# Latent attention: order of a score pass and the context's transposes, and operands filled up from 32 to 128 rows

## The reference, cut to what matters

```python
q = (x @ W_q).reshape(b, t, 16, 8).transpose(0, 2, 1, 3)
lat = x @ W_dkv                                   # 32 features
lat = (lat - mean) * rsqrt(var + 1e-5) * ln_gamma + ln_beta
k = (lat @ W_uk).reshape(b, t, 16, 8).transpose(0, 2, 1, 3)
v = (lat @ W_uv).reshape(b, t, 16, 8).transpose(0, 2, 1, 3)
q, k = apply_rope(q), apply_rope(k)
scores = einsum('bhqd,bhkd->bhqk', q, k) / sqrt(8)
attn = softmax(where(causal, scores, -inf))
out = einsum('bhqk,bhkd->bhqd', attn, v).transpose(0, 2, 1, 3).reshape(b, t, 128) @ W_o
```

## Time and profile before

| what | us |
|---|---|
| median of three runs | 1756.51 (1756.41 to 1758.79) |
| the profiled execution | 1753.8 |
| its span, first to last instruction | 1752.0 |
| latent layer, from the first copy to latT to the last one (15 steps) | 589.5 to 1008.3 |

### The profile page before, as it was taken

The page is one execution under the profiler, slowest core; times in us unless marked ns, Lnnn a source line. Parts: engine busy times, 40 slices in busy tenths (PEclk is TensorE's granted clock), DMA queues, the critical chain, the costliest instruction groups (busy, mean ns, idle before and its releaser), DMA issues.

```text
span 1752.0 us, 33687 instructions
## 1 busy us (share of the span) xinstructions
PE 1506.7 (86%) x12538; PEld 1127.1 (64%) x12538; DVE 1014.7 (58%) x2795; ACT 729.0 (42%) x1281; POOL 252.7 (14%) x514
## 2 busy tenths in 40 slices
PE   5999999994099499999999995499998899998977
PEld 3666666662098266666666654366665899997667
DVE  4666777764065355665666546734444566664856
ACT  0444444333065134434343333266666455553322
POOL 0000000010601212212121101200000000000423
PEclk7999999995599568887897867789999899998989
DMA  9000000000122100000000000000000000000001
GB/s 304 13 1 1 1 1 2 1 1 2 58 62 68 61 4 7 7 4 7 4 7 4 1 1 1 1 1 2 2 1 2 1 1 2 1 2 1 1 16 34
DMA packets 32673, 30.39 MB, mean 17 GB/s; under 512 B 4536, under 2 KB 29312, under 8 KB 31872
## 3 DMA queue, kind: packets, MB, share of 16 engines
q1 hardware_dynamic: 30464, 24.05, 4.5%
q0 software_dynamic: 2048, 4.20, 0.8%
HBM read 18.01 MB, written 10.22 MB: 16 GB/s over the span
## 4 chain that ended last, share of the span: by engine, by line
PE 72%; DVE 10%; POOL 5%; ACT 5%; issue 4%; DMA 2%; SPq 0%; POOLq 0%; DVEq 0%; ACTq 0%
PE S L355 12%; PE O L1559 7%; PE O L425 6%; PE S L341 5%; PE A L329 4%; PE S L344 4%; PE A L310 3%; PE A L330 3%; ACT probs L647 3%; PE O L429 3%; PE S L1541 2%; PE A L446 2%; PE S L1542 2%; PE S L1543 2%; PE O L383 2%
## 5 line engine op out<-in xcount | busy, mean ns | idle before, releaser
L647 ACT ACTIVATE probs<-S 128x1024 f32<-128x1024 f32 x288 | 290.8, 1026 | 217.8 <-PE S L355 211.9
L823 DVE TENSOR_REDUCE nm<-S 128x4 f32<-128x1024 f32 x128 | 151.8, 1215 | 88.7 <-PE S L355 88.5
L156 POOL TENSOR_TENSOR ve<-mv,eps 128x2 f32<-128x2 f32 x112 | 26.5, 237 | 1112.4 <-DVE mv L148 1112.4
L1627 ACT ACTIVATE probs<-S,eb 128x256 f32<-128x256 f32 x256 | 107.7, 474 | 117.8 <-PE S L1543 117.8
L654 ACT COPY OT<-O 128x512 f32<-128x512 f32 x96 | 56.3, 587 | 206.2 <-PE O L429 206.2
L425 PE MATMUL O<-probs,V 128*32 128x256 f32 x1536 | 134.8, 426 | 4.8 <-ACT probs L647 3.3
L1559 PE MATMUL O<-ew,probs 128*128 128x128 f32 x1024 | 138.1, 278 | 0.3 <-ACT probs L1627 0.2
L329 PE MATMUL A<-hi,spread 128*128 128x256 f32 x384 | 117.8, 335 | 18.0 <-DVE lo L802 8.8
L355 PEld LDWEIGHTS S<-QM,KS 32*128 32x128 f32 x1024 | 87.3, 223 | 69.8 <-issue 69.8
L1559 PEld LDWEIGHTS O<-ew,probs 128*128 128x128 f32 x1024 | 125.1, 192 | 5.2 <-ACT probs L1627 3.5
L355 PE MATMUL S<-QM,KS 32*128 32x256 f32 (+1 forms) x1024 | 127.3, 353 | 0.0
(11 more groups left out here) (338 smaller groups left out, 3116.4 us busy)
## 6 DMA issues: line engine op xcount, KB each, us to landing
ew<-in_w SPq DMA_DIRECT2D x2, 2048.0 KB, 10.1
moe_rows<-zeros SPq DMA_DIRECT2D x1, 2944.0 KB, 12.9
xin<-moe_rows SPq DMA_DIRECT2D x23, 128.0 KB, 2.6
ew<-in_w SPq DMA_DIRECT2D x2, 1024.0 KB
out<-X SPq DMA_DIRECT2D x16, 128.0 KB, 1.8
moe_made<-ctx_sb SPq DMA_DIRECT2D x12, 128.0 KB, 1.8
moe_made<-ctxT SPq DMA_DIRECT2D x11, 128.0 KB, 1.8
probs<-in_spread SPq DMA_DIRECT2D x1, 1024.0 KB, 5.2
```

What stands on the lines that cost most here:

```text
L647: act.activation(c.probs[:, n].rearrange("p b g l -> p b (g l)"), c.S[:, n % 2], ACT.Exp if soft else ACT.Tanh, scale=self.scale).then_inc ...
L823: dve.tensor_reduce(c.nm[:, 1, 2 * pr:2 * pr + 2, 2 * u:2 * u + 2], slot.rearrange("p b (g k) -> p b g k", g=2), AX.X, ALU.max, negate=Tru ...
L1627: act.activation(w["h"][:, x % 2, j], c.S[:, x % 2, bank, col:col + L], ACT.Relu, bias=w["b1"][:, x * self.NJ + j:x * self.NJ + j + 1]).th ...
```

## The change

It does four things, all in the latent layer. First, `latent_T` writes to bank 1 of O and not to bank 0, and the wait of `maxima` for ACT's copy of it stands ahead of the third group (the first that writes bank 1) and not ahead of the first. Second, on PE pass1(5) stands ahead of the context's transposes. Third, the two query projections change places: bank 1 of A first. Fourth, the tiles uk, uv and latT have 128 partitions; rows 32 to 127 are set to zero once at the start by six memsets on DVE, and the key and value matmuls read all 128 rows. The weight loads, the folding and ACT's copy still touch rows 0 to 31 alone, and the loads of uk and uv are issued two places later among the other loads of their group.

```diff
@@ latent_T (PE)
-                mm = pe.transpose(c.O[0:LAT, 0, t * P:(t + 1) * P], w["lat"][:, t, :], c.ident[:])
+                mm = pe.transpose(c.O[0:LAT, 1, t * P:(t + 1) * P], w["lat"][:, t, :], c.ident[:])
@@ maxima (PE)
-            if has_front and kind == "latent":
-                pe.wait_ge(e["latt"].sem, e["latt"].at(s + 1))
             for g in range(G):
+                if g == 2 and has_front and kind == "latent":
+                    pe.wait_ge(e["latt"].sem, e["latt"].at(s + 1))
                 for t in range(T):
@@ latent_step (PE)
             pass1(k, par, 4)
+            pass1(k, par, 5)
             if has_tail:
                 ctx_transposes(k - 1)
-            pass1(k, par, 5)
             if has_front:
+                projections(k + 1, 1, (0,))
                 projections(k + 1, 0, (0,))
-                projections(k + 1, 1, (0,))
                 latent_T(k + 1, nxt)
             maxima(k, has_front)
@@ latent_copy (ACT)
-            act.copy(w["latT"][:], c.O[0:LAT, 0, 0:L]).then_inc(e["latt"].sem, 1)
+            act.copy(w["latT"][0:LAT, :], c.O[0:LAT, 1, 0:L]).then_inc(e["latt"].sem, 1)
@@ build: tiles and loads
-        w1 = dict(wq=sb("wq1", [P, 2, P]), uk=sb("uk1", [LAT, 2, P]), uv=sb("uv1", [LAT, P]),
+        w1 = dict(wq=sb("wq1", [P, 2, P]), uk=sb("uk1", [P, 2, P]), uv=sb("uv1", [P, P]),
...
-                             lat=sb("lat", [P, T, LAT]), latT=sb("latT", [LAT, L]))
+                             lat=sb("lat", [P, T, LAT]), latT=sb("latT", [P, L]))
...
+        load("l1", w1["uk"][0:LAT], d["uk1"])
+        load("l1", w1["uv"][0:LAT], d["uv1"])
@@ start of DVE's program
+            for rows in (slice(LAT, 2 * LAT), slice(2 * LAT, P)):
+                dve.memset(w1["uk"][rows], 0.0).then_inc(made, 1)
+                dve.memset(w1["uv"][rows], 0.0).then_inc(made, 1)
+                dve.memset(w1["latT"][rows], 0.0).then_inc(made, 1)
```

More of the change, by code:

```diff
@@ L2283, in build @@
                              lrstd=sb("lrstd", [P, T]), lminus=sb("lminus", [P, T]), lnm=sb("lnm", [P, T]),
-                             lat=sb("lat", [P, T, LAT]), latT=sb("latT", [LAT, L]))
+                             lat=sb("lat", [P, T, LAT]), latT=sb("latT", [P, L]))
         w1["wqk"] = [w1["wq"], w1["uk"]]
-        for dst, name in ((w1["wq"], "wq1"), (w1["uk"], "uk1"), (w1["uv"], "uv1"), (w1["dkv"], "dkv1"), (w1["wo"], "wo1")):
+        for dst, name in ((w1["wq"], "wq1"), (w1["dkv"], "dkv1"), (w1["wo"], "wo1")):
             load("l1", dst[:], d[name])
+        load("l1", w1["uk"][0:LAT], d["uk1"])
+        load("l1", w1["uv"][0:LAT], d["uv1"])
         load("l1", w1["gamma"][:], d["gamma1"].rearrange("(n o) -> n o", o=1))
@@ L2373, in build @@
         experts0.loaded = loaded["moe0"], 16 * len(loads["moe0"])
-        N_MADE = 25
+        N_MADE = 31
         def fold_products(pe):
@@ L2380, in fold_products @@
             for sw in range(2):
-                pe.matmul(c.S[:, 0, 1, NE * sw:NE * sw + NE], w1["uk"][:, sw, :], w1["beta_all"][:, 0:NE], start=True, stop=True)
-            pe.matmul(c.S[:, 0, 1, P:2 * P], w1["beta_all"][:], w1["uv"][:], start=True, stop=True).then_inc(folded["beta_ps"], 1)
+                pe.matmul(c.S[:, 0, 1, NE * sw:NE * sw + NE], w1["uk"][0:LAT, sw, :], w1["beta_all"][:, 0:NE], start=True, stop=True)
+            pe.matmul(c.S[:, 0, 1, P:2 * P], w1["beta_all"][:], w1["uv"][0:LAT], start=True, stop=True).then_inc(folded["beta_ps"], 1)
         def fold(dve):
@@ L2389, in fold @@
             dve.tensor_copy(w1["bv"][:], c.S[:, 0, 1, P:2 * P]).then_inc(folded["latent_folded"], 1)
-            dve.tensor_scalar(w1["uk"][:], w1["uk"][:], w1["gamma"][:, 0:1], None, ALU.mult).then_inc(folded["latent_folded"], 1)
-            dve.tensor_scalar(w1["uv"][:], w1["uv"][:], w1["gamma"][:, 0:1], None, ALU.mult).then_inc(folded["latent_folded"], 1)
+            dve.tensor_scalar(w1["uk"][0:LAT], w1["uk"][0:LAT], w1["gamma"][:, 0:1], None, ALU.mult).then_inc(folded["latent_folded"], 1)
+            dve.tensor_scalar(w1["uv"][0:LAT], w1["uv"][0:LAT], w1["gamma"][:, 0:1], None, ALU.mult).then_inc(folded["latent_folded"], 1)
         experts0.fold_products, experts0.fold = fold_products, fold
```

## The result

The changed kernel takes 1681.12 us (median of four runs, 1675.60 to 1685.51) against 1757.65 for the kernel before (four runs, the three of the table above and 1763.98): a ratio of 0.9576, 95% interval 0.9541 to 0.9610. Forecast was 1695 with a range of 1685 to 1714. The profile after is of the quickest of the four runs (1675.60).

The account below looks back on a forecast made before the run. PE was taken to bound the kernel, with its clock falling in the latent layer. Falls 56.8 us plus maxima 4.8 made 61.6, taken from the median 1756.5: 1695 us, range 1685 to 1714.

Parts of the forecast that it names:

- The falls: Latent layer: 32-row projections let PE's clock drop to 0.50; zero rows remove 12 drops, 56.8 us; chance 0.78.
- some falls stay: Rival: 32-row score passes or PE's longer wait for lo still drop the clock; half left, 1723 us, chance 0.12.
- no fall goes: Rival: the clock follows something other than rows in use; only the maxima gain, 1747 to 1752 us, chance 0.07.
- the low clock stays longer: Rival: moved transposes or filled-up matmuls delay the clock's rise in latent steps; 31 us more, 1787, chance 0.03.
- The wait of the maxima: At L383 the maxima start after M instead of the latT copy: 0.32 us per step, 4.8 in all.
- PE's own gain: Around L310, fewer changes between 128-row and 32-row matmuls: 0 to 0.3 us per step, taken as 0.
- pass1(5): Score pass ahead of the context's transposes fills PE's 0.34 us idle, but DVE's row maxima bound it: gain 0.
- The cover on ACT: 0.32 us between ACT's later ctxT copy and lat's wait for POOL; if gone, at worst 0.3 per step, 4.5 us.
- The early step: Latent step 618.6 to 648.6, begun at low clock: left as it is; an earlier rise would give up to 6.3 us.
- the fourteenth step's fall: Latent step 1008.3 to 1037.9: without its clock drop it goes from 29.6 to 23.75 us, 5.8 less.
- the 13 steps: Latent layer, 648.6 to 1008.3, latT copy to latT copy: 359.7 us before, forecast to shorten by 55.2.

Follow-up runs that it names:

- the zero rows alone: The kernel before with only the filled-up tiles, loads and memsets; order, bank and waits as before: 1687.36 us, ratio 0.9613.
- the order alone: The changed kernel with the latent layer's key and value matmuls reading rows 0 to 31 again: 1752.93 us, ratio 0.9998.
- the cut rope layer: The changed kernel with the rope layer's keys and values contracting over 32 of 128 rows: 1749.58 us.
- 64 rows: The changed kernel with the latent layer's keys and values contracting over 64 rows instead of 128: 1696.92 us.

## Why the prediction was right in its cause and short in its sum

**The falls: right, and shown.** 32-row projections are the cause; the zero rows alone, the order alone and the cut rope layer say so in three ways. The rivals "some falls stay", "no fall goes" and "the low clock stays longer" are out for the changed kernel. The first lives in the kernels between: with 64 rows 2 steps of 13 fall.

**The wait of the maxima: right.** M to QM went from 1.33 to 1.04 us, 0.29 where 0.32 was forecast; the step gives back 0.34 with the wait put back.

**PE's own gain: taken as 0, measured 0.15 per step.** The prediction bounded it by 0 to 0.3 and said that it "would only lengthen PE's wait for lo". This step failed in its mechanism. It read DVE's chain from QM to lo as without a gap, since none of its eight rows shows idle time. There was one, too short to be printed. V ends at 709.32 + 0.48 = 709.80 and the residual L884 starts at 709.85, behind PE's output L463, which ends at 709.10 + 0.71 = 709.81:

```profile
709.32 0.48 DVE L760 TENSOR_TENSOR V<-O,bv 128x128 f32<-128x128 f32 x2
709.85 0.42 DVE L884 TENSOR_TENSOR res<-O,X 128x256 f32<-128x256 f32 x1
```

```profile
709.10 0.71 PE L463 MATMUL O<-wo,ctxT 128*128 128x128 f32 x4
```

After the change V and the residual start 0.40 apart (781.52, 781.92) and not 0.53, and the residual no longer waits: it starts before V's end at 782.00. The line of L884 as a whole hides this. It counts 16 waits before and 4 after, and none of the 16 is in the two steps at full clock; they stand in the steps with a fall and at the ends of the rope and the latent layer. So 0.13 of the 0.15 us arrives here: full rows bring PE's output earlier by 0.12 (3.90 us behind the maxima, 4.02 before), and DVE was waiting for it. From the start of QM to that of lo it is 5.18 us before (705.82 to 711.00) and 5.03 after, 5.12 in the step shown. With 64 rows V and the residual are 0.73 apart in all steps at full clock but one, and with 32-row keys 0.62, which is why their steps are longer. With the values on 32 rows PE is another 0.10 us ahead and the step stays at 23.24: only from there on is the prediction's sentence true.

**pass1(5): taken as 0, measured 0.07** per step at full clock, together with the exchange of the query projections. The prediction had DVE as the bound here. It was not quite: its maxima 4 and 5 start 1.15 us apart with the pass late and 1.11 with it early, so 0.04 of the 0.07 is another wait too short to be printed. The cover on ACT held (0.38 us).

**The early step: taken as 0, the first two gave 7.3 us** where 0.6 was forecast. In size this is the term that failed most. "I leave it as it is" put the rise of the clock at 635.1, where the kernel before had it; after, it stays up from 616.9 on, with one short rise ahead of that. Before:

```profile
589.50:635.10 45.60, 38.79 (x172) 24.13 (x172) 20.30 (x37) 8.65 (x13) 4.06 (x9) 0.50 0.01 3
635.10:648.60 13.50, 12.73 (x120) 8.22 (x120) 8.41 (x16) 5.75 (x11) 1.63 (x6) 1.00 0.01 1
```

And after:

```profile
585.80:616.90 31.10, 24.83 (x101) 17.38 (x100) 15.63 (x26) 3.47 (x7) 3.20 (x6) 0.56 0.02 5
616.90:637.60 20.70, 19.51 (x193) 12.43 (x192) 13.04 (x28) 10.72 (x17) 2.48 (x8) 1.00 0.00 1
```

The prediction had the price (6.3) as a bound only. It is hardly chance: in the six profiles with full keys and no added work the first two steps take 50.4 to 53.6 us, in the four with 32- or 64-row keys 54.6 to 59.1. Which products bring the rise forward was not tested.

**The ends.** The last stretch gave 10.7 us; the fourteenth step's fall is 5.8 of them. The other 4.9, and the 3.7 ahead of the layer, are not tied to the change: the last stretch takes 48.7 to 53.1 us with full keys and 49.5 to 59.4 without, and the first copy to latT lies anywhere from 585.8 to 591.3 in the ten profiles without added work, though nothing ahead of it differs but the memsets and the place of two small loads. What sets the place of the low stretches there was not settled.

So of the 16.6 us between sum and measurement (78.2 - 61.6), 6.7 were the early step, 2.0 the 13 steps, and some 8 the places of low stretches in one pair of executions (4.9 + 3.7 - 0.7). With the first two in the sum the forecast would have been 1756.5 - 61.6 - 6.7 - 2.0 = 1686, just inside the range. The medians moved by 76.5 us here and by 73.3 where the changed kernel was seen again, so 3 to 6 us beyond those 70.3 are not tied to a cause. The range had no room for them: its low end counted 4.5 for PE and most of the early step, and nothing for scatter, while the kernel before alone ran from 1737 to 1764 us in 24 executions on several chips, and 1767 in one more. Three that lay within 2.4 us had looked like a steady kernel.

## What to carry to other kernels

Where the granted clock falls although PE is busy, look at how many rows its matmuls use there, and compare a stage that does the same work over 128 rows; zero rows are a cheap trial. A chain of short instructions without printed idle time can still wait: where one reads another engine's result, set its start against the end of that result, and the distance of the two starts against a step in which it can't wait, before a gain on the other engine is set to 0. If a stretch at the low clock is part of the kernel, one profile and three close times do not give its scatter, and the range must.

## What the runs showed that was not expected

- The clock fell with PE busy 0.90 of 0.90 us and stood at 0.50 while it was busy 17.10 of 17.10, in the rope layer over 32 rows; in the latent layer, in one profile each, 0 steps of 13 fell with keys over 128 rows, 2 with 64, 5 with 32-row keys and full values, 11 and 13 with 32 rows throughout.
- Rows that are zero count: filled with nothing but zeros they hold the clock (1.00 over 306.5 us) as the rope layer's real data do (1.00 over 320).
- The key projections of a step (four instructions) over 32 or 64 rows between 128-row matmuls take 0.14 us more from start to start than over 128 rows (1.05 and 1.06 against 0.91), though their printed durations are alike. Values on 32 rows behind a 32-row score pass are quicker than full ones: the output follows the maxima by 3.80 us and not 3.90.
- Products that nobody reads, in PE's waits, raised the mean clock of the 20 us ahead of a layer from 0.50 to 0.92 and shortened its first step by 6.4 us (27.3 to 21.0).
